# Attention and routed experts: layernorm folded into the router's logits, residual kept in x's rows, orders of three engines changed

## The reference

```python
# _L0_xattn_ref(ctx, layernorm(x), Wq, Wk, gamma_raw): b, n = 4, 512
sim = einsum('bhnd,bhmd->bnm', Q, K) / (sqrt(d) * H)
threshold = top_k(sim, 153)[0][:, :, -1:]           # the 153rd largest of each row
A = sigmoid(sim) * (sim >= threshold)
A = (A + swapaxes(A, -1, -2)) * 0.5
x = x + (1.0 - gamma) * layernorm(x) + gamma * A    # x1 in this text
# _L0_ffn_ref(layernorm(x1), ...): 2048 tokens, 16 experts
logits = xn @ router_weight.T + router_bias
top_val, top_idx = top_k(logits, 4);  top_val = softmax(top_val)
gate_up = einsum('th,ehd->etd', xn, gate_up_proj) + gate_up_proj_bias
out = einsum('etd,edh->eth', (up + 1.0) * glu, down_proj) + down_proj_bias
x = x1 + (out * router_scores).sum(experts)
```

## Time and profile before

| | us |
|---|---|
| median of 3 runs | 910.04 |
| lowest and highest run | 905.74, 911.15 |
| profiled execution, its own time | 910.28 |
| profiled execution, its span | 908.5 |

### The profile page before, as it was taken

The page is one execution under the profiler, slowest core; times in us unless marked ns, Lnnn a source line. Parts: engine busy times, 40 slices in busy tenths (PEclk is TensorE's granted clock), DMA queues, the critical chain, the costliest instruction groups (busy, mean ns, idle before and its releaser), DMA issues.

```text
span 908.5 us, 16718 instructions
## 1 busy us (share of the span) xinstructions
PE 776.5 (85%) x3558; PEld 627.6 (69%) x3559; DVE 593.4 (65%) x1063; ACT 404.5 (45%) x663; POOL 316.7 (35%) x351
## 2 busy tenths in 40 slices
PE   5355463548899999999999999999999999999993
PEld 2124242537678888878888887887788878888882
DVE  3667697696755755776766757667857475765541
ACT  2997868732333424354343525434443243352221
POOL 1330555574632323333242424333332322333231
PEclk9755575556999999999999999999999999999996
DMA  8501131117373641854727455477548354723231
GB/s 275 200 0 47 47 47 47 49 48 220 94 204 82 175 106 38 211 171 102 228 46 229 110 165 171 112 201 209 147 121 229 55 136 128 218 53 63 52 66 22
DMA packets 70626, 111.80 MB, mean 123 GB/s; under 512 B 29878, under 2 KB 32182, under 8 KB 70518
## 3 DMA queue, kind: packets, MB, share of 16 engines
q1 hardware_dynamic: 32454, 74.22, 23.9%
q0 software_dynamic: 18336, 36.26, 20.2%
q10 hardware_dynamic: 19728, 0.15, 1.2%
HBM read 83.78 MB, written 28.90 MB: 124 GB/s over the span
## 4 chain that ended last, share of the span: by engine, by line
PE 59%; DMA 9%; issue 4%; POOL 4%; DVE 2%; ACT 2%; ACTq 1%; DVEq 1%; SPq 0%; POOLq 0%
PE gate_up_ps L844 33%; PE bank L844 20%; DMA xg<-xn_rows,gslot 5%; PE bank L826 3%; PE bank L834 3%; POOL out_dram L437 2%; POOL slot_rows L393 2%; DMA out_dram<-xn 1%; DMA bgu<-n_gate_up_proj_bias_dram 1%; ACT w L653 1%; DMA slot_rows<-payload,slot_i 1%; DMA raw_w<-in_L_ffn_down_proj_dram 1%; DVE hl L1029 1%; ACT yb L635 0%; DMA gslot<-slot_rows 0%
## 5 line engine op out<-in xcount | busy, mean ns | idle before, releaser
L844 PE MATMUL gate_up_ps<-w,xh 128*128 (+1 forms) x1152 | 363.9, 397 | 0.0
L437 POOL DMA_INDIRECT out_dram<-yb,aslot x72 | 131.2, 1822 | 424.9 <-ACT yb L635 410.1
L844 PEld LDWEIGHTS gate_up_ps<-w,xh 128*128 128x128 f32 x1152 | 212.5, 189 | 40.8
L844 PE MATMUL gate_up_ps<-w,xl 128*128 (+1 forms) x576 | 226.3, 393 | 0.0
L844 PE MATMUL bank<-w,hh 128*128 (+1 forms) x576 | 181.0, 396 | 7.0 <-DVE hl L1029 6.5
L628 ACT ACTIVATE sg<-gc 128x512 f32<-128x512 f32 x72 | 45.6, 634 | 221.5 <-DVE gc L1039 221.5
L1035 DVE TENSOR_TENSOR gu<-gate_up_ps,bgu 128x1024 f32<-128x1024 f32 x72 | 88.1, 1224 | 71.7 <-PE gate_up_ps L844 70.4
L844 PEld LDWEIGHTS bank<-w,hh 128*128 128x128 f32 x576 | 108.0, 190 | 35.3 <-issue 13.5
L1029 DVE TENSOR_TENSOR hl<-bank,hh 128x512 fp32r<-128x512 f32 x72 | 49.5, 688 | 116.9 <-ACT hh L622 116.9
L844 PEld LDWEIGHTS gate_up_ps<-w,xl 128*128 128x128 f32 x576 | 108.7, 189 | 23.6
L622 ACT CAST hh<-bank 128x512 fp32r<-128x512 f32 x72 | 42.3, 587 | 160.4 <-PE bank L834 159.2
(11 more groups left out here) (205 smaller groups left out, 800.7 us busy)
## 6 DMA issues: line engine op xcount, KB each, us to landing
raw_w<-_L_ffn_gate_up_proj_dram SPq DMA_DIRECT2D x64, 512.0 KB, 4.2
raw_w<-in_L_ffn_down_proj_dram SPq DMA_DIRECT2D x64, 256.0 KB, 5.7
bgu<-n_gate_up_proj_bias_dram SPq DMA_DIRECT2D x16, 512.0 KB, 6.9
x_sb<-in_x_dram SPq DMA_DIRECT2D x4, 1024.0 KB, 12.1
xn_rows<-xn SPq DMA_DIRECT2D x4, 1024.0 KB, 6.8
out_dram<-xn SPq DMA_DIRECT2D x4, 1024.0 KB, 5.3
xg<-xn_rows,gslot POOLq DMA_INDIRECT x74, 5.2
out_dram<-yb,aslot POOLq DMA_INDIRECT x72, 4.8
```

The source lines that it names most:

```text
L437: pool.indirect_dma_start(out_v, bass.IndirectOffsetOnAxis(aslot[:, k, 0:1], 0), yb[:, k % 2, :], None, bounds_check=TOKENS - 1, oob_is_er ...
L844: last = nc.tensor.matmul(out_ps, lhs[:, rows], w[:, bass.ds(buf, 1), part, c, cols].rearrange("p a d -> p (a d)"), start=(m == 0), stop=( ...
```

## The change

x1 is written into `x_sb` in place, so that the buffer `x1` goes; the sum with the bias and the store to the output use the same rows. TensorE transposes x1 itself, not its normalised rows, and the router multiplies it as it is. With r2 the inverse deviation and b2 = -mean * r2 of a row, the logits are r2 * (x1 . w) + (b2 * rsum + bias), where rsum is the sum of the router's weights over the channels (five new small steps: a product with ones on TensorE, a copy, and for each batch four `shift` and four `logit` instructions of 16 elements in place of one of 64). The normalised rows, which the experts gather, are made after `gates`.

Orders: on ScalarE `norm` is parted in `across` (copies of the transposes, with the square root between the second and the third) and `norm`, behind `deviations` and `gates`; `exponentials` moves from the second round of the search to ahead of the first. On TensorE `ctx_across(2)` and `count_ok(0)` stand ahead of `project(2)`, and `project(3)` behind the transposes of A. On VectorE `add_bias` stands behind the rows of x1, the scale and shift behind `thresholds` and `first_guess`, and the payload ahead of `dense`; four instructions at L1107 become one over 128x2048, and four at L1190 one. ScalarE's first split of expert 1's weights waits for the store of the last output rows.

```diff
-                sp.dma_start(out_v[rows, :].rearrange("(r p) h -> p r h", p=P), base_out[:]).then_inc(S["acc_out"], 16)
+                sp.dma_start(out_v[rows, :].rearrange("(r p) h -> p r h", p=P), x_sb[:, b * RT:(b + 1) * RT, :]).then_inc(S["acc_out"], 16)
...
+            def across(b):
+                if b:
+                    act.wait_ge(S["logit_ps"], b)
+                for r in range(RT):
+                    act.wait_ge(S["xt_ps"], RT * b + r + 1)
+                    nc.scalar.copy(xn2T[:, r, :], ps_t[r % 2]).then_inc(S["xt_done"], 1)
+                    if r == 1:
+                        act.wait_ge(S["var2"], b + 1)
+                        nc.scalar.activation(sd[:], mv[:, :, 1], ACT.Sqrt, bias=eps_c[:]).then_inc(S["sd2"], 1)
+
             def norm(b):
-                act.wait_ge(S["var2"], b + 1)
-                nc.scalar.activation(sd[:], mv[:, :, 1], ACT.Sqrt, bias=eps_c[:]).then_inc(S["sd2"], 1)
                 act.wait_ge(S["aff2"], b + 1)
                 if b:
-                    act.wait_ge(S["acc_out"], 16 * b)
-                    act.wait_ge(S["xt_ps"], RT * b)
-                for r in range(RT):
-                    nc.scalar.activation(xn2[:, r, :], x1[:, r, :], ACT.Identity,
+                    act.wait_ge(S["xn2_out"], 16 * b)
+                for r in range(RT):
+                    nc.scalar.activation(xn2[:, r, :], x_sb[:, RT * b + r, :], ACT.Identity,
                                          bias=b2[:, r:r + 1], scale=r2[:, r:r + 1]).then_inc(S["xn2_done"], 1)
-                if b:
-                    act.wait_ge(S["logit_ps"], b)
-                for r in range(RT):
-                    act.wait_ge(S["xt_ps"], RT * b + r + 1)
-                    nc.scalar.copy(xn2T[:, r, :], ps_t[r % 2]).then_inc(S["xt_done"], 1)
...
-                    if it == 1:
+                    if it == 0:
                         exponentials(b - 2)
...
-                norm(b)
+                across(b)
                 if b + 2 < NB:
                     deviations(b + 2)
                 if b + 1 < NB:
                     gates(b + 1)
+                norm(b)
...
+                act.wait_ge(S["acc_out"], 16 * NB)
...
+                ctx_across(b)
                 project(b)
                 scores(b, 0, RT)
+            for c in range(HC):
+                last = nc.tensor.matmul(ps_rw[:, 0:E], ones[:], rwT[:, c * E:(c + 1) * E], start=(c == 0), stop=(c == HC - 1))
+            last.then_inc(S["rsum_ps"], 1)
+            ctx_across(2)
+            count_ok(0)
             project(2)
-            count_ok(0)
             scores(2, 0, 2)
             for b in range(NB):
 
                 if b == 1:
-                    project(3)
+                    ctx_across(3)
                 pe.wait_ge(S["a_done"], RT * (b + 1))
                 if b:
                     pe.wait_ge(S["scT_done"], b)
...
-                pe.wait_ge(S["x1_done"], RT * (b + 1))
-                if b:
-
-                    pe.wait_ge(S["payload_done"], b)
-                    pe.wait_ge(S["bo_done"], RT * b)
                 for r in range(RT):
                     i = RT * b + r
-                    pe.wait_ge(S["xn2_done"], i + 1)
+                    pe.wait_ge(S["x1_done"], RT * b + min(r + 3, RT))
                     if i >= 2:
                         pe.wait_ge(S["xt_done"], i - 1)
                     for c in range(HC):
-                        last = T_(ps_t[r % 2][:, c * P:(c + 1) * P], xn2[:, r, c * P:(c + 1) * P], ident[:])
+                        last = T_(ps_t[r % 2][:, c * P:(c + 1) * P], x_sb[:, i, c * P:(c + 1) * P], ident[:])
                     last.then_inc(S["xt_ps"], 1)
+                    if b and r == 1:
+
+                        pe.wait_ge(S["payload_done"], b)
+                        pe.wait_ge(S["bo_done"], RT * b)
...
-                dve.wait_ge(S["xn2_out"], 16 * b + 16)
+                dve.wait_ge(S["xn2_done"], RT * b + r + 1)
                 dve.wait_ge(S["bd_ps"], RT * b + r + 1)
-                V.tensor_tensor(base_out[:, r, :], ps_bias[b][r], x1[:, r, :], ALU.add).then_inc(S["bo_done"], 1)
+                V.tensor_tensor(x_sb[:, RT * b + r, :], ps_bias[b][r], x_sb[:, RT * b + r, :], ALU.add).then_inc(S["bo_done"], 1)
...
+            dve.wait_ge(S["rsum_ps"], 1)
+            link(V.tensor_copy(rsum[:], ps_rw[:, 0:E]))
...
-                for r in range(RT):
-                    send(V.scalar_tensor_tensor(out=x_sb[:, RT * b + r, :], in0=A[:, r, :], scalar=gam[:, 2:3],
-                                                in1=x_sb[:, RT * b + r, :], op0=ALU.mult, op1=ALU.add))
-                join()
+                rows = slice(RT * b, RT * (b + 1))
+                link(V.scalar_tensor_tensor(out=x_sb[:, rows, :], in0=A[:], scalar=gam[:, 2:3], in1=x_sb[:, rows, :],
+                                            op0=ALU.mult, op1=ALU.add))
+                for r in range(RT):
+                    dve.wait_ge(S["at_ps"], RT * b + r + 1)
+                    V.scalar_tensor_tensor(out=x_sb[:, RT * b + r, :], in0=ps_t[r % 2], scalar=gam[:, 2:3],
+                                           in1=x_sb[:, RT * b + r, :], op0=ALU.mult, op1=ALU.add).then_inc(S["x1_done"], 1)
                 if b:
                     for r in range(RT):
                         add_bias(b - 1, r)
-                if b:
-
-                    dve.wait_ge(S["xn2_done"], RT * b)
-                    dve.wait_ge(S["bo_done"], RT * b)
-                for r in range(RT):
-                    dve.wait_ge(S["at_ps"], RT * b + r + 1)
-                    V.scalar_tensor_tensor(out=x1[:, r, :], in0=ps_t[r % 2], scalar=gam[:, 2:3],
-                                           in1=x_sb[:, RT * b + r, :], op0=ALU.mult, op1=ALU.add).then_inc(S["x1_done"], 1)
                 dve.wait_ge(S["x1_done"], RT * (b + 1))
                 for r in range(RT):
-                    send(V.bn_stats(st[:, r, :], x1[:, r, :]))
+                    send(V.bn_stats(st[:, r, :], x_sb[:, RT * b + r, :]))
...
-                dve.wait_ge(S["sd2"], b + 1)
-                link(V.reciprocal(r2[:], sd[:]))
-                link(V.tensor_tensor(b2[:], mv[:, :, 0], r2[:], ALU.mult))
-                V.tensor_scalar(b2[:], b2[:], -1.0, None, ALU.mult).then_inc(S["aff2"], 1)
...
+                dve.wait_ge(S["sd2"], b + 1)
+                link(V.reciprocal(r2[:], sd[:]))
+                link(V.tensor_tensor(b2[:], mv[:, :, 0], r2[:], ALU.mult))
+                V.tensor_scalar(b2[:], b2[:], -1.0, None, ALU.mult).then_inc(S["aff2"], 1)
+                dve.wait_ge(S["aff2"], b + 1)
+                for r in range(RT):
+                    send(V.scalar_tensor_tensor(out=shift[:, r, :], in0=rsum[:], scalar=b2[:, r:r + 1], in1=rb_sb[:],
+                                                op0=ALU.mult, op1=ALU.add))
+                join()
                 dve.wait_ge(S["logit_ps"], b + 1)
-                link(V.tensor_tensor(logit[:], ps_logit.rearrange("p (r e) -> p r e", e=E),
-                                     rb_sb[:].unsqueeze(1).broadcast_to([P, RT, E]), ALU.add))
+                for r in range(RT):
+                    send(V.scalar_tensor_tensor(out=logit[:, r, :], in0=ps_logit[:, r * E:(r + 1) * E], scalar=r2[:, r:r + 1],
+                                                in1=shift[:, r, :], op0=ALU.mult, op1=ALU.add))
+                join()
...
-                link(V.tensor_tensor(hotv[:].rearrange("p r k e -> p (r k) e"), hot[:].rearrange("p r k e -> p (r k) e"),
-                                     score[:].rearrange("p r k -> p (r k)").unsqueeze(2).broadcast_to([P, RT * TOP_K, E]),
-                                     ALU.mult))
-                V.tensor_reduce(dense[:], hotv[:].rearrange("p r k e -> p r e k"), AX.X, ALU.add).then_inc(S["dense_done"], 1)
-                dve.wait_ge(S["dense_done"], b + 1)
                 dve.wait_ge(S["rank_ps"], b + 1)
                 link(V.tensor_tensor(pos[:], ps_rank.rearrange("p (r e) -> p r e", e=E),
                                      slot0_e[:].unsqueeze(1).broadcast_to([P, RT, E]), ALU.add))
-                for r in range(RT):
-                    send(V.tensor_tensor(hotv[:, r], hot[:, r], pos[:, r, :].unsqueeze(1).broadcast_to([P, TOP_K, E]), ALU.mult))
-                join()
+                link(V.tensor_tensor(hotv[:], hot[:], pos[:].unsqueeze(2).broadcast_to([P, RT, TOP_K, E]), ALU.mult))
...
+                link(V.tensor_tensor(hotv[:].rearrange("p r k e -> p (r k) e"), hot[:].rearrange("p r k e -> p (r k) e"),
+                                     score[:].rearrange("p r k -> p (r k)").unsqueeze(2).broadcast_to([P, RT * TOP_K, E]),
+                                     ALU.mult))
+                V.tensor_reduce(dense[:], hotv[:].rearrange("p r k e -> p r e k"), AX.X, ALU.add).then_inc(S["dense_done"], 1)
```

More of the change, by code:

```diff
@@ L160, in xattn_moe_kernel @@
         rb_sb = sb("rb_sb", [P, E])
+        rsum = sb("rsum", [P, E])
+        shift = sb("shift", [P, RT, E])
```

(26 more changed lines are left out.)

4 lines of the change are left out of this document (3 added, 1 removed).

## The result

| | before | changed |
|---|---|---|
| median, us | 909.91 (4 runs, 905.74 to 911.15) | 898.22 (4 runs, 895.62 to 904.15) |
| profiled execution | as above | 900.14, span 898.3 |

The ratio is 0.9879, 95% interval 0.984 to 0.9918: 11 us less by that ratio (11.7 by the medians); 900.4 was forecast. There are also chips on which the kernel before takes 921 us. What follows is about the first kind of chip unless it is said.

The account below looks back on a forecast made before the run. The chain of waits through the batches, setting how early TensorE's busy tile loop starts, was taken as the bound. Payload 3 and all behind it 9.6 us earlier: 910.28 to 900.7, less 0.24, 900.4; range 896.0 to 905.5.

Parts of the forecast that it names:

- Start: Batch 0: VectorE's 5.91 us wait for the count goes; x1 gains some 2.3 us, ScalarE's search(1) about as much.
- Behind a search: From router products to exponentials, reordered as copies, gates, norm, exponentials: in batch 0 VectorE goes on 7.5 us earlier.
- Of the 4.38 us wait nothing is left: VectorE's wait for project(3) ahead of x1 of batch 1 vanishes; x1 ends at 107.4 instead of 114.8.
- The merged instruction: VectorE's one-for-four instruction lasts about 2.25 us, saves 0.5; ScalarE stands some 2.4 us in a search instead of 0.85.
- Rival (a): Merged instruction lets GpSimd through as often as four did: 3.1 us more gain, 897.3; chance 0.17.
- Payload 3 to tile 4: Scatters, landing, table and gather of tile 4 follow the last payload at unchanged distance, all 9.6 us earlier.
- rival (b): Last store or load chain becomes the bound: 902.9, up to 906 with small losses at handovers; chance 0.19.
- a sign of being wrong: In the profile after, GpSimd waiting for the last store would show the forecast wrong, as (b).
- Landing 9.03 us later at 230.1; GpSimd needs it at 230.5: Last store, issued at 221.05, lands before GpSimd needs it behind its scatters; margin 0.4 us.
- The sum: Everything shifts 9.6 us earlier: 910.28 to 900.7 on the profiled execution, 900.4 as median.
- (c): Nothing reaches the end: the clock or a wait inside the tile loop takes it back, about 908 to 911; chance 0.07.

Follow-up runs that it names:

- third-round experiment: Changed kernel with the routed scores' copy in the third round of ScalarE's search instead of the fifth: 895.65 us, ratio 0.9853 to the kernel before.
- store experiment: Changed kernel with the last store issued ahead of the last wait of expert 1's loads: 897.50 us, ratio 0.9838 to the kernel before.

## Why the prediction was right, and where it was not

**Start: right.** The wait for the count is 0.30 us, and taking the move back or making it alone gives 2.4 and 2.3 us where 2.3 were forecast.

**Behind a search: right in batch 0, too small behind it.** From zero the exponentials of batch 0 come to VectorE 7.6 us sooner (7.5 forecast), those of batch 1 8.4 (7.3) and those of batch 2 8.9 (6.3). The term that was mis-sized is the stretch from a first router product to the last copy, put at 5.9 us from the earlier trace rows: in batch 1 the product starts at 112.86 and the last copy ends at 116.3, 3.4 us, eight products taking 1.04 us where they took 1.89. The stages say why, first of the changed kernel, then of the kernel before (TensorE alone, columns as above):

```profile
105.00:110.00 5.00, 3.27 (x8) 1.00 0.31 97
110.00:115.00 5.00, 4.62 (x32) 1.00 1.48 46
```

```profile
114.00:118.00 4.00, 3.55 (x9) 1.00 0.02 1
118.00:122.00 4.00, 0.21 (x2) 1.00 0.02 1
122.00:128.00 6.00, 4.78 (x27) 0.57 0.74 94
```

Before, TensorE did next to nothing from 118 to 122, waiting for the normalised rows, and the router's products found the clock mostly at its lower level, 1.2 GHz. Now it goes from the scores straight to the transposes of x1, at 2.4 GHz. `project(3)`, put at 3.8 us, took 1.9 at a granted clock of 1.00 (0.50 before). So VectorE, not ScalarE, brings up the end of batches 1 and 2: it has no idle time ahead of their exponentials.

**"Of the 4.38 us wait nothing is left": wrong as a wait, right as a time.** VectorE idles 7.43 us there; its own bias sums no longer fill that time, and the transposes stand behind the bias rows, which wait for the copy of the routed scores at 97.48. x1 ends at 63.9 from zero, and the forecast's 107.4 is 63.8 from the zero of its own trace. The third-round experiment shows that the place of that copy was worth another 2.6 us in the trace.

**The merged instruction: right.** 2.35 us (2.25 forecast), one GpSimd operation of 2.30 beside it, ScalarE 2.34 and 2.47 us in searches 2 and 3 (2.4). The Trainium skill (Advanced Engine Details and Errata, Mode Summary) names instructions in two-port mode as blocking GpSimd; it does not name those with two inputs, and the 2.30 us row shows one of them doing it. Rival (a)'s mechanism is out, but its price of 3.1 us for two searches without the block is near what taking the instruction apart gave in the trace, 2.7. The merged instruction is thus a part of the change that costs more than the 0.4 us of VectorE's time it saves.

**Payload 3 to tile 4: rival (b) happened, inside the forecast's time.** GpSimd waited for the store, which the prediction gave as a sign of being wrong, and its first add came 6.71 us after its last scatter. "Landing 9.03 us later at 230.1; GpSimd needs it at 230.5" misread the row: in the chain before, too, the piece of 9.03 us ends where a scatter of GpSimd does (237.58), and the profile's list of DMA issues gives that store (its last number) 10.5 us to landing:

```profile
out_dram<-xn SPq DMA_DIRECT2D x1, 1024.0 KB, 10.5
```

With 10.5 the forecast's own sum has the store 1.1 us late. Then three things moved, counted from zero. The payload came 1.2 us sooner than forecast (164.5 for 165.7). The store was issued 2.4 us later (179.8 for 177.4): its loads followed a first gather that was 1.0 us sooner, but took 3.4 us longer, of which 1.6 are a landing (7.43 against 5.86) and 1.8 an issue (2.23 against 0.43). And GpSimd was let go up to 11.2 us after the issue. The term that failed is the distance from the payload to the gather of tile 4, forecast as unchanged: 28.3 us before, 30.7 now. The store experiment takes 1.8 of the 2.4 us back. The slower gather (1.7 us) was in no term.

**The sum.** 9.6 forecast, all of it in the batches; 10.1 in the two profiled executions, made of 10.6, less 4.2, 1.6 in the loop and 2.2 of a luckier start. Payload 3 was right within 1.0 us; on the way there the exponentials of batch 2 were off by 2.6. Without the start the two traces differ by 8.0, 1.6 under the forecast, so that the total comes so near is in part luck. The times say 11 us, by their interval 7.5 to 14.6; how many of those runs had the slow first products is not known, so what the change alone is worth on this kind of chip is not known better than that. That a chip exists on which the gain is lost was in no rival: (c) put it inside the tile loop, with a chance of 0.07.

## What to carry to other kernels

Count traces from the last event that the change hardly touches, or the 2 us by which two executions of one kernel differ ahead of it will be taken for its effect. When producers are made faster, list every chain that ends in the same consumer with its margin, and read a landing from the list of DMA issues: the chain thought to have 0.4 us in hand had none. When an engine stands, look whether its next step was released by what it stood for; here the 6.71 us cost nothing by themselves. A small instruction that engine after engine waits for is worth its place in a queue more than its length: the copy moved by two rounds bought 2.6 us in the trace, the normalised rows moved back cost 7 in time.

## What the hardware showed that was not expected

- There are chips on which the kernel before is 11 us slower; the changed kernel, measured on one of two, is 21.6 us slower, and its gain is gone. In its trace ScalarE stands 8 to 14 us, three times up to 246, for a signal of TensorE whose work had long ended, each time while GpSimd's scatters are issued or just after (a scatter stretch ends at 123.1, the copy starts at 125.42; 243.1 and 245.89). VectorE's chained small instructions slow down there too, from 0.04 us between two of them to 0.55, until the same moment (from 125.36 on they are at 0.03 again):

```profile
122.56 0.16 DVE L996 SCALAR_TENSOR_TENSOR tied<-above,tied 128x4 f32<-128x4 f32 x1
123.27 0.17 DVE L997 TENSOR_SCALAR above<-above 128x4 f32<-128x4 f32 x1 [0.55 <-DVE tied L996]
123.96 0.16 DVE L998 SCALAR_TENSOR_TENSOR above<-tied,above 128x4 f32<-128x4 f32 x1 [0.52 <-DVE above L997]
```

  The scatters are beside it in time; that they cause it was not tried, and what differs in the chips stays open. A kernel that puts the scatters elsewhere would tell.
- One [128x2] GpSimd operation, 0.19 us alone, lasts 2.30 us beside a VectorE instruction of 2.35 us with two inputs in SBUF, and 2.31 on the second chip.
- An issue of a load on SyncE took 2.23 us (0.43 as a rule), and the store behind it waited for that too. Loads of 256 and 512 KB stood ahead of it, but they did in the trace before as well, where it took 0.44; why is open.
- TensorE's first eight score products take either 3.79 us or about 6 in executions of the same kernels, at a granted clock of 1.00 in both.
